# Normalising the next image on GpSimd in place of VectorE during attention

## The chip, the cores and the metric

The kernel runs on one core of one Trainium2 chip. Its time is the device time of one execution in microseconds (us), and the number compared is the median of several runs. The engines are TensorE (PE in the profile; PEld is its weight load), VectorE (DVE), ScalarE (ACT), GpSimd (POOL) and SyncE (SP), which issues most of the DMAs. Each engine works through its own queue in order; they wait for one another on semaphores.

## The reference

Sixteen images of 192 channels by 32 by 32 go through a convolutional attention block, then as 1024 tokens of 192 channels each through causal attention over 6 heads, and then through a mixture of 4 experts, of which each token takes 2. Every step adds its result to its input. What the change touches is the first line of it:

```python
mu = jnp.mean(x, axis=(1, 2, 3), keepdims=True)
var = jnp.mean((x - mu) ** 2, axis=(1, 2, 3), keepdims=True)
xn = (x - mu) * jax.lax.rsqrt(var + EPS) * ln_g + ln_b
Q = _proj(xn, wq_p, bq_p, wq_d, bq_d)   # 3x3 convolution per channel behind a head-wise product
...
out = jnp.einsum('bhnc,bhcd->bhnd', V, attn)
...
return jnp.einsum('bcij,oc->boij', out, w_f) + b_f[None, :, None, None] + xn
# then, on tokens:
t = t + _L1_attn_ref(_ln_t(t), L1_attn_W_qkv, L1_attn_W_proj, L1_attn_b_proj)
t = t + _L1_ffn_ref(_ln_t(t), L1_ffn_gate_w, L1_ffn_gate_b, L1_ffn_w1, L1_ffn_b1, L1_ffn_w2, L1_ffn_b2)
```

`ln_g` and `ln_b` have one value for each channel and pixel; the mean and the variance are one number for an image.

## The kernel before

A loop over the 16 images computes the convolution block and the attention of one image after the other; behind it a loop over 67 blocks of 512 routed rows computes the experts. An image takes about 133 us. The change lies in the loop over images.

**Stages of an image.** TensorE convolves the padded image (`conv`, L1720) from `ring`, which holds shifted copies of it. The padded image `xpad` (96 partitions, two halves of the channels, rows of 34 pixels) is written to DRAM by SyncE (`write_scratch`, L343) and read back in 36 shifted loads (`load_pairs`, L352). After the channel attention and its projection come the token norm, queries, keys and values, and then the token attention.

**The token attention** is an order written out by hand: 48 units, 8 chunks of 128 queries (`qc`, 0 to 7) times 6 heads (`h`), numbered n = 6 qc + h. For a unit, TensorE computes the scores (L1843, mask L1845), VectorE their negated row maximum (`score_max`, L1094), ScalarE the exponentials with row sums (L1543), TensorE transposes them (`blocks`, L1855), ScalarE or VectorE copies them out of PSUM (L1557, L1107). Scores run two or three units ahead. After h = 5 of a chunk TensorE multiplies by the values for four heads (`four_heads`, L1877), and in the next chunk at h = 1 for the last two (`two_heads`, L1887).

**The inverse sums.** VectorE takes the reciprocals of a chunk's row sums at the next chunk's h = 0 (`inverse_sums`, L1115). GpSimd copies them wide in two instructions (`inverse_wide`, L765 and L766), TensorE transposes these right behind `two_heads` (`norms`, L1895), ScalarE copies the result (L1565), VectorE multiplies (`weighted`, L1124), and at h = 3 TensorE projects (`output_projection`, L1904). "The third chunk's norms" below are those of qc = 2, executed in chunk qc = 3, and so on.

**The next image's norm** is woven into this attention on VectorE, by unit: statistics at n = 6 to 12, the deviation at 15, the variance at 18, with one small matrix product each on TensorE. GpSimd takes the reciprocal root (`image_rstd`, L390) behind the inverse sums of qc = 2. Then VectorE runs `gain` (L941), (x - mean) x ln_g in place, for either half at n = 20 and 22, and `shift` (L954), x rstd + ln_b into the inside of `xpad`, at n = 25 and 27. Each is one scalar_tensor_tensor over 96x1024 elements. SyncE's next steps after its loads for the attention are the two scratch writes and the 36 ring loads; the convolution of the next image starts behind unit 47. GpSimd copies `xpad` to `xn` (`unpad_image`, L328) at the next image's start.

In the last image (number 15, counted from 0) there is no next image: none of this work exists, and GpSimd instead splits expert weights behind the inverse sums (`split_behind`, L773 and L776).

Of the kernel before, what the change touches and what calls it, by code (L numbers as in the profile page):

```python
# [10 lines left out]
ALU = mybir.AluOpType  # L11
# [8 lines left out]
def hybrid_block_kernel(nc, x, ln_g, ln_b, conv_w, conv_bias_row, conv_taps, conv_bias, alpha_rows, w_f_t, b_f,  # L20
                        w_qkv_a, w_qkv_b, w_proj, w_proj_t, b_proj, gate_w_a, gate_w_b, gate_b, w1_a, w1_b, b1_t,
                        w2, b2, out):
    B, C, SH, SW = x.shape
# [51 lines left out]
    with ExitStack() as ctx:  # L75
# [29 lines left out]
        x_sb = at("x_sb", [HALF, 2, N], F32, 2 * (PAIRS - 1) * RING)  # L105
# [42 lines left out]
        img = sb("img", [HALF, 8])  # L148
# [122 lines left out]
        def sem(name):  # L271
            return ctx.enter_context(nc.semaphore(name))
# [30 lines left out]
        bcur_sb, xT_ps, xT_hi, xT_lo, up_ps, gelu_sb, lo_sb, down_ps, acc_ps, y_acc, yrow_sb = sems(  # L303
            "bcur_sb xT_ps xT_hi xT_lo up_ps gelu_sb lo_sb down_ps acc_ps y_acc yrow_sb")
        outT_ps, outs_sb, comb = sems("outT_ps outs_sb comb")
        w_hi, front_sb = sem("w_hi"), sem("front_sb")
        xgt_ld = [sem(f"xgt_ld{n}") for n in range(3)]
        cur_ld = [sem(f"cur_ld{n}") for n in range(2)]
        yrow_st = [sem(f"yrow_st{n}") for n in range(2)]
# [8 lines left out]

        def interior(h):
            return xpad[:, h, 0:PW * (SH + 2)].rearrange("p (a b) -> p a b", b=PW)[:, 1:SH + 1, 1:SW + 1]  # L320

        def unpad_image(pool, i):

# [64 lines left out]
        def image_rstd(pool, i):  # L388
            pool.wait_ge(img_veps, i + 1)
            nc.gpsimd.tensor_tensor(img[:, 5:6], img[:, 4:5], minus_half[0:HALF, 0:1], ALU.pow).then_inc(img_rstd, 1)  # L390
# [63 lines left out]
        def passage(i):  # L454
            return PASSAGES[0 if i + 1 < B else 1]

        def pass_bank(t):
            return 4 + t % 2
# [228 lines left out]
        def _(pool):  # L687
# [132 lines left out]
            def output_bias(i, j):  # L820
# [2 lines left out]
                g.tensor_tensor(t_sb[:, ch, :], t_sb[:, ch, :],  # L823
                                b2p_bc[:, :].unsqueeze(1).to_broadcast([P, TPC, CE]), ALU.add).then_inc(tb_sb, 1)

            for i in range(B):
                unpad_image(pool, i)
                if i:
                    send(i - 1, 0, 3)
                token_rstd(i, 0)  # L830
                if i:
                    send(i - 1, 3, 5)
                token_rstd(i, 1)
                if i:
                    send(i - 1, 5, 6)
                pool.wait_ge(qk_hi, NQ * i + PAIR_GROUPS)
                for j in range(2):
                    load_queries(g, 0, j, 0, QKh)
                    load_queries(g, 0, j, 2, QKh)
                pool.wait_ge(qk_lo, NQ * i + PAIR_GROUPS)  # L840
                for j in range(2):
                    load_queries(g, 0, j, 1, QKl)
                if i:
                    send(i - 1, 6, NC)
                output_bias(i, 0)
                for qc in range(NC):
                    inverse_wide(i, qc)
                    if qc == 0:
                        output_bias(i, 1)
                    if qc == 2 and i + 1 < B:  # L850
                        image_rstd(pool, i + 1)
                    if qc == TPC:
                        token_rstd2(i, 0)
                    if i + 1 == B:
                        split_behind(qc)
                if i + 1 < B:
                    token_rstd2(i, 1)
# [47 lines left out]
        def _(dve):  # L905
# [28 lines left out]
            def variance(i, at_bank):  # L934
                dve.wait_ge(stat_ps, 2 * i + 2)
                v.tensor_scalar(img[:, 4:5], bank(at_bank)[0:HALF, 1:2], 1e-5, None, ALU.add).then_inc(img_veps, 1)

            def gain(i, h):
                if i == 0 and h == 0:
                    dve.wait_ge(w_ld["ln"], 32)  # L940
                v.scalar_tensor_tensor(out=x_sb[:, h, :], in0=x_sb[:, h, :], scalar=img[:, 0:1],  # L941
                                       in1=lng[:, h, :], op0=ALU.subtract, op1=ALU.mult).then_inc(xg_sb, 1)

            def shift(i, h):
                if h == 0:
                    dve.wait_ge(img_rstd, i + 1)
                    dve.wait_ge(xg_sb, 2 * (i + 1))
                    if i:

                        dve.wait_ge(xn_flat, 2 * i)  # L950
                        for h2 in range(2):
                            dve.wait_ge(scr_w[h2], 16 * i)
                rows = lambda a: a.rearrange("p (a b) -> p a b", b=SW)
                v.scalar_tensor_tensor(out=interior(h), in0=rows(x_sb[:, h, :]), scalar=img[:, 5:6],  # L954
                                       in1=rows(lnb[:, h, :]), op0=ALU.mult, op1=ALU.add).then_inc(xn_sb, 1)

            for q in range(4):
                stats(0, q)
# [1 line left out]
            deviation(0, 4)  # L960
            variance(0, 4)
            for h in range(2):
                gain(0, h)
            dve.wait_ge(setup_pool, 4)
            for h in range(2):
                shift(0, h)
            dve.wait_ge(setup_pool, 7)
            v.tensor_copy(ident_g[:, 0:HALF], ident[0:HALF, 0:HALF])
            v.tensor_tensor(block_mask[:, :], mask_wide[:, 0:2 * W], mask_wide[:, 2 * W:P], ALU.max)
# [344 lines left out]
            for i in range(B):  # L1314
                conv_qk(i, 0)
                if i:
                    route(i - 1, 0)
                else:
                    finish_setup(0)
                conv_qk(i, 1)  # L1320
                if i:
                    route(i - 1, 1)
                else:
                    finish_setup(1)
                channel_logits(i, 0)
                if i:
                    route(i - 1, 2)
                else:
                    finish_setup(2)
                channel_attention(i, 0)  # L1330
                if i:
                    route(i - 1, 3)
                else:
                    finish_setup(3)
                conv_qk(i, 2)
                transposed_attention(i, 0)
                if i:
                    route(i - 1, 4)
                else:
                    finish_setup(4)  # L1340
                conv_qk(i, 3)
                channel_logits(i, 1)
                channel_attention(i, 1)
                if i:
                    route(i - 1, 5)
                transposed_attention(i, 1)
                if i:
                    route(i - 1, 6)
                else:
                    finish_setup(5)  # L1350

                for k in range(TPC):
                    channel_mixed(i, k)
                    if k:
                        first_stats(i, k - 1)
                first_stats(i, TPC - 1)
                channel_mixed(i, TPC)
                first_stats(i, TPC)
                normed(i, 0)
                for k in range(TPC + 1, NC - 1):  # L1360
                    channel_mixed(i, k)
                    first_stats(i, k)
                low_channels(i, 0)
                channel_mixed(i, NC - 1)
                first_stats(i, NC - 1)
                low_qk(i, 0)
                normed(i, 1)
                for n in range(1, QK_FIRST):
                    low_qk(i, n)
                low_channels(i, 1)  # L1370
                for n in range(QK_FIRST, NQ):
                    low_qk(i, n)

                image_steps = {6: lambda: stats(i + 1, 0), 8: lambda: stats(i + 1, 1), 10: lambda: stats(i + 1, 2),
                               12: lambda: (stats(i + 1, 3), partition_mean(i + 1)),
                               15: lambda: deviation(i + 1, pass_bank(passage(i).stat[0])),
                               18: lambda: variance(i + 1, pass_bank(passage(i).stat[1])),
                               20: lambda: gain(i + 1, 0), 22: lambda: gain(i + 1, 1),
                               25: lambda: shift(i + 1, 0), 27: lambda: shift(i + 1, 1)}
                def query_chunk(qc, stage):  # L1380
                    if stage == 0:
                        inverse_sums(i, qc)
                    if stage == 2:
                        weighted(i, qc)
                    if stage == 4:
                        attended(i, qc)
                    if stage == 5:
                        second_stats(i, qc)

                for n in SCORED_FIRST:  # L1390
                    score_max(i, n)
                for n, (qc, h) in enumerate(SOFT):
                    for m in SCORED[n]:
                        score_max(i, m)
                    blocks_out(i, n)
                    if qc:
                        query_chunk(qc - 1, h)
                    if i + 1 < B and n in image_steps:
                        image_steps[n]()
                    if i + 1 == B and n == 40:  # L1400
                        second_normed(i, 0)
                for stage in range(H):
                    query_chunk(NC - 1, stage)
# [748 lines left out]
```

## Time and profile before

| what | value |
|---|---|
| median of 3 runs | 3315.94 us (3314.32 to 3317.31) |
| profiled execution | 3319.14 us, span of its trace 3317.3 us |
| TensorE busy | 3075.1 us (93%) |
| VectorE busy | 2204.9 us (66%) |
| ScalarE busy | 1871.7 us (56%) |
| GpSimd busy | 875.3 us (26%) |
| mean granted TensorE clock | 0.986 of full |

Times inside the trace are counted from the span's start. The loop over images ends near 2225 us; the experts fill the rest. Image 14's attention runs from about 2000 to 2080 us, image 15's from about 2139 to 2222 us. "Releaser" is what ended an engine's idle time, read from semaphore events. The ends of matrix products are modelled, so starts are the firmer numbers.

### The profile page before, as it was taken

To read this page: it belongs to the slowest core of one execution; us is meant where nothing else is said; L and a number is where in the kernel's file an instruction comes from. 1 tells how busy PE (TensorE), PEld (TensorE's weight loads), DVE (VectorE), ACT (ScalarE), POOL (GpSimd) and SP (SyncE) were. 2 spreads that over 40 slices of the span, in tenths; PEclk is the share of its full clock that TensorE was granted. 3 is DMA by queue.
4 is the path that set the end of the run, shared out by engine and by line. 5 is a ranking of instruction groups with operands and counts; after the bars stand their busy time and mean duration, and the time that the engine had idled before them with its cause. 6 is when DMAs were issued, how large, how long until landed. Compare 5 with 4: busy or idle time off the path is not lost.

```text
span 3317.3 us, 72524 instructions
## 1 busy us (share of the span) xinstructions
PE 3075.1 (93%) x26642; PEld 2349.3 (71%) x26642; DVE 2204.9 (66%) x5632; ACT 1871.7 (56%) x3996; POOL 875.3 (26%) x1142
## 2 busy tenths in 40 slices
PE   4999999999989999999999999988999999999995
PEld 1666667666666676666766666667888888888884
DVE  3777677677776777777767777664565655655653
ACT  0647466475474664745746547464555555555553
POOL 2121303313123032131330322352133233233223
PEclk9999999999999999999999999999999999999997
DMA  7547445454464554644545447334667767767673
GB/s 178 142 113 174 123 115 149 123 156 119 124 165 115 136 138 115 173 115 126 150 124 148 127 113 183 100 130 147 187 219 221 216 202 217 216 209 225 202 215 118
DMA packets 256517, 519.83 MB, mean 157 GB/s; under 512 B 70919, under 2 KB 161991, under 8 KB 246521
## 3 DMA queue, kind: packets, MB, share of 16 engines
q1 hardware_dynamic: 222878, 453.58, 48.7%
q0 software_dynamic: 29184, 59.81, 6.0%
q8 instruction: 217, 3.56, 0.4%
q10 hardware_dynamic: 4107, 1.81, 0.3%
q14 instruction: 131, 1.07, 0.1%
HBM read 242.82 MB, written 117.71 MB: 109 GB/s over the span
## 4 chain that ended last, share of the span: by engine, by line
PE 67%; DVE 14%; issue 10%; ACT 3%; POOL 2%; DMA 2%; SPq 1%; DVEq 0%; ACTq 0%; POOLq 0%
PE ps L2042 13%; PE ps L1855 9%; PE ps L2058 9%; PE ps L1720 5%; PE ps L1843 5%; PE ps L2063 5%; PE ps L1804 3%; PE ps L1877 3%; PE ps L1887 2%; PE ps L2018 2%; PE ps L1812 2%; ACT p_sb L1543 2%; DVE minus_max L1094 1%; PE ps L1895 1%; PE ps L2027 1%
## 5 line engine op out<-in xcount | busy, mean ns | idle before, releaser
L1094 DVE TENSOR_REDUCE minus_max<-ps 128x1 f32<-128x128 f32 (+7 forms) x768 | 571.7, 750 | 246.9 <-PE ps L1845 231.3
L1543 ACT ACTIVATE p_sb<-ps,minus_max 128x128 f32<-128x128 f32 (+7 forms) x768 | 569.3, 741 | 41.0 <-DVE minus_max L1094 37.0
L1855 PE MATMUL ps<-ident,p_sb 128*128 128x128 f32 x3456 | 532.1, 279 | 44.5 <-ACT p_sb L1543 19.1
L1665 ACT ACTIVATE g<-ps,bcur 128x512 f32<-128x512 f32 x402 | 276.8, 688 | 447.4 <-PE ps L2042 441.4
L1428 DVE TENSOR_TENSOR g_lo<-g,g_hi 128x512 fp32r<-128x512 f32 x402 | 282.2, 702 | 361.4 <-ACT g_hi L1666 361.4
L1557 ACT ACTIVATE PT<-ps 128x512 f32<-128x512 f32 (+3 forms) x768 | 396.8, 517 | 134.4 <-PE ps L1855 125.3
L1855 PEld LDWEIGHTS ps<-ident,p_sb 128*128 128x128 f32 x3456 | 371.8, 142 | 99.4 <-ACT p_sb L1543 38.4
L2058 PE MATMUL ps<-w_all,g_hi 128*128 x1608 | 437.1, 352 | 1.6 <-DVE y_rows L1452 1.6
L1843 PE MATMUL ps<-KS,QS 96*128 96x512 f32 (+3 forms) x1152 | 393.6, 401 | 21.2 <-ACT p_sb L1543 19.6
L1720 PE MATMUL ps<-ring,wconv 125*32 125x512 f32 (+1 forms) x3072 | 357.1, 605 | 16.6 <-DMA ring<-padded_scratch 16.6
L817 POOL DMA_INDIRECT routed_rows<-xhat,slot x256 | 253.8, 991 | 345.6 <-issue 345.6
L878 POOL DMA_INDIRECT got<-expert_rows,slot x256 | 258.2, 1008 | 327.1 <-issue 267.9
L765 POOL COPY inverse_wide<-inverse_sums 128x192 f32<-128x192 f32 x128 | 44.2, 345 | 1046.7 <-DVE inverse_sums L1115 1046.7
L2063 PE MATMUL ps<-w_all,g_lo 128*128 x1608 | 292.6, 264 | 0.3 <-DVE g_lo L1428 0.3
L2063 PEld LDWEIGHTS ps<-w_all,g_lo 128*128 128x128 f32 x1608 | 289.8, 188 | 3.1 <-DVE g_lo L1428 1.2
L2058 PEld LDWEIGHTS ps<-w_all,g_hi 128*128 128x128 f32 x1608 | 264.4, 191 | 26.6 <-DVE y_rows L1452 2.3
L2042 PE MATMUL ps<-X_hi,cur 128*128 128x512 f32 x780 | 256.6, 410 | 18.9 <-issue 12.1
L1666 ACT ACTIVATE g_hi<-ps,bcur 128x512 fp32r<-128x512 f32 x402 | 273.4, 680 | 0.0
L1843 PEld LDWEIGHTS ps<-KS,QS 96*128 96x128 f32 x1152 | 196.9, 195 | 68.9 <-ACT p_sb L1543 41.7
L2042 PE MATMUL ps<-X,cur 128*128 128x512 f32 x780 | 244.9, 395 | 0.0
L1720 PEld LDWEIGHTS ps<-ring,wconv 125*32 125x32 f32 (+1 forms) x3072 | 93.5, 111 | 208.5 <-issue 193.1
L1107 DVE COPY PT<-ps 128x128 f32<-128x128 f32 (+3 forms) x384 | 184.9, 481 | 68.5 <-PE ps L1855 68.3
(293 smaller groups left out, 5462.7 us busy)
## 6 DMA issues: line engine op xcount, KB each, us to landing
ring<-padded_scratch SPq DMA_DIRECT2D x576, 204.0 KB
cur<-w_all SPq DMA_DIRECT2D x65, 1536.0 KB, 7.1
routed_rows<-zero_rows SPq DMA_DIRECT2D x67, 384.0 KB, 5.1
xgt<-routed_rows SPq DMA_DIRECT2D x67, 384.0 KB, 4.5
expert_rows<-y_rows SPq DMA_DIRECT2D x67, 384.0 KB, 3.1
padded_scratch<-xpad SPq DMA_DIRECT2D x32, 435.0 KB, 3.6
x_sb<-x SPq DMA_DIRECT2D x16, 768.0 KB, 5.4
KS<-QKh SPq DMA_DIRECT2D x128, 96.0 KB
```

Of the source, the lines that this page charges most:

```text
L1094: v.tensor_reduce(nmx[:, qc, h:h + 1], score_place(n), AX, ALU.max, negate=True).then_inc(mx_sb, 1)
L1428: v.tensor_tensor(g_lo[:, n % 2, :], g32[:, n % 2, :], g_hi[:, n % 2, :].bitcast(F32), ALU.subtract).then_inc(lo_sb, 1)
L1543: a.activation(p_sb[n % NP][:, 0:P * (qc + 1)], score_place(n), ACT.Exp, bias=nmx[:, qc, h:h + 1], accum_out=ls[:, qc, h:h + 1]).then_inc( ...
L1557: a.activation(PT[h][:, k0:k0 + nb, :], bank(pass_bank(t))[:, 0:P * nb].rearrange("p (k q) -> p k q", q=P), ACT.Copy).then_inc(PT_act, 1)
L1665: a.activation(g32[:, n % 2, :], bank(n % 2), ACT.Gelu, bias=b1)
L1666: a.activation(g_hi[:, n % 2, :], bank(n % 2), ACT.Gelu, bias=b1).then_inc(gelu_sb, 1)
L1720: last = t.matmul(bank(2 * (r % 2) + nh)[W * j:W * (j + 1), :], wconv[s][0:KROWS[s], h, c0:c0 + W], rhs, start=s == 0, stop=s == 1, skip_g ...
L1843: t.matmul(o[:, k0:k0 + keys], QS[0:96, qc // TPC, h, P * (qc % TPC):P * (qc % TPC + 1)], KS[0:96, h, k0:k0 + keys], start=True, stop=k0 + ...
L1855: last = t.transpose(bank(pass_bank(piece))[:, P * k:P * (k + 1)], p_sb[n % NP][:, P * (k0 + k):P * (k0 + k + 1)], ident[:, :])
L2042: last = t.matmul(bank(n % 2), w[:, W1L * part + P * j:W1L * part + P * (j + 1)], act_part[:, :], start=m == 0, stop=m == 4)
L2058: t.matmul(bank(acc_bank(r, tt))[:, 0:2 * C], g_hi[:, n % 2, P * tt:P * (tt + 1)], w2j, start=j == 0, stop=False, skip_group_check=True)
L2063: last = t.matmul(bank(acc_bank(r, tt))[:, 0:C], g_lo[:, n % 2, P * tt:P * (tt + 1)], w2j[:, 0:C], start=False, stop=j == J - 1, skip_grou ...
```

## The change

The four VectorE instructions for images 1 to 15 become six on GpSimd; for image 0 they stay (`first_gain`, `first_shift`). On GpSimd, `gain` stands behind the inverse sums of qc = 2 and the reciprocal root: for either half one tensor_scalar, (x - mean) x rstd in place, and one tensor_tensor, times ln_g in place, with a new semaphore `x_unit` between them. `shift` stands behind the inverse sums of qc = 3: for either half one tensor_tensor that adds ln_b and writes the inside of `xpad`. The waits of the old `shift` go along; each half now waits for its own scratch write.

```diff
+            def gain(i):
+
+                pool.wait_ge(xstat, 2 * i + 2)
+                pool.wait_ge(img_rstd, i + 1)
+                for h in range(2):
+                    g.tensor_scalar(x_sb[:, h, :], x_sb[:, h, :], img[:, 0:1], img[:, 5:6], ALU.subtract, ALU.mult
+                                    ).then_inc(x_unit, 1)
+                for h in range(2):
+                    pool.wait_ge(x_unit, 2 * (i - 1) + h + 1)
+                    g.tensor_tensor(x_sb[:, h, :], x_sb[:, h, :], lng[:, h, :], ALU.mult).then_inc(xg_sb, 1)
+
+            def shift(i):
+                pool.wait_ge(xg_sb, 2 * (i + 1))
+                pool.wait_ge(xn_flat, 2 * i)
+                for h in range(2):
+                    pool.wait_ge(scr_w[h], 16 * i)
+                    g.tensor_tensor(interior(h), image_rows(x_sb, h), image_rows(lnb, h), ALU.add).then_inc(xn_sb, 1)
...
                     if qc == 2 and i + 1 < B:
                         image_rstd(pool, i + 1)
+                        gain(i + 1)
+                    if qc == 3 and i + 1 < B:
+                        shift(i + 1)
...
-                               18: lambda: variance(i + 1, pass_bank(passage(i).stat[1])),
-                               20: lambda: gain(i + 1, 0), 22: lambda: gain(i + 1, 1),
-                               25: lambda: shift(i + 1, 0), 27: lambda: shift(i + 1, 1)}
+                               18: lambda: variance(i + 1, pass_bank(passage(i).stat[1]))}
```

## Rows read from the trace of the kernel before

**Rows 1.** The page: busy us (share of the span); the chain by engine
```profile
PE 3075.1 (93%) x26642; PEld 2349.3 (71%) x26642; DVE 2204.9 (66%) x5632; ACT 1871.7 (56%) x3996; POOL 875.3 (26%) x1142
...
PE 67%; DVE 14%; issue 10%; ACT 3%; POOL 2%; DMA 2%; SPq 1%; DVEq 0%; ACTq 0%; POOLq 0%
```

**Rows 2.** Windows (images 14, 14, 15): length, busy us of each engine, clock, DMA
```profile
2020.10:2029.20 9.10, 8.29 (x96) 6.28 (x94) 7.82 (x15) 8.03 (x20) 0.53 (x2) 1.00 0.00 1
2029.20:2039.90 10.70, 9.98 (x120) 7.90 (x116) 10.16 (x21) 8.82 (x20) 1.29 (x3) 1.00 0.56 148
...
2175.20:2183.00 7.80, 7.42 (x100) 5.84 (x99) 5.98 (x15) 6.31 (x13) 4.37 (x6) 1.00 0.01 2
```

**Rows 3.** Chain of waits in image 14: start us, us, what
```profile
2024.51 1.19 DVE x_sb L941
```

**Rows 4.** Timeline of TensorE, image 14: start us, us, what, idle before
```profile
2020.10 0.44 PE L1895 MATMUL ps<-ident,inverse_wide 128*128 128x128 f32 x2
...
2027.40 0.56 PE L1843 MATMUL ps<-KS,QS 96*128 96x512 f32 x2 [0.15 <-ACT p_sb L1543]
...
2028.65 0.64 PE L1887 MATMUL ps<-PT,v_sb 128*32 128x128 f32 x16
2029.22 0.44 PE L1895 MATMUL ps<-ident,inverse_wide 128*128 128x128 f32 x2
...
2032.06 0.50 PE L1904 MATMUL ps<-wproj_a,aT 128*128 128x196 f32 x2
...
2039.90 0.44 PE L1895 MATMUL ps<-ident,inverse_wide 128*128 128x128 f32 x2
```

**Rows 5.** Timeline of TensorE, image 15
```profile
2157.14 0.44 PE L1895 MATMUL ps<-ident,inverse_wide 128*128 128x128 f32 x2
...
2165.62 0.64 PE L1887 MATMUL ps<-PT,v_sb 128*32 128x128 f32 x16
2171.11 0.69 PE L1895 MATMUL ps<-ident,inverse_wide 128*128 128x128 f32 x2 [4.84 <-POOL inverse_wide L766]
...
2175.16 0.50 PE L1904 MATMUL ps<-wproj_a,aT 128*128 128x196 f32 x2
...
2183.00 0.44 PE L1895 MATMUL ps<-ident,inverse_wide 128*128 128x128 f32 x2
```

**Rows 6.** Groups by form, VectorE: shapes, count, busy us, mean ns, idle before
```profile
L954 DVE SCALAR_TENSOR_TENSOR xpad<-x_sb,img,lnb 96x1024 f32<-96x1024 f32 x32 | 40.8, 1277 | 0.1
L941 DVE SCALAR_TENSOR_TENSOR x_sb<-x_sb,img,lng 96x1024 f32<-96x1024 f32 x32 | 40.7, 1273 | 2.0 <-DMA lnb<-ln_b 2.0
```

**Rows 7.** Timeline of GpSimd, image 14
```profile
2019.36 0.58 POOL L390 TENSOR_TENSOR img<-img,minus_half 96x1 f32<-96x1 f32 x1
2027.99 0.35 POOL L765 COPY inverse_wide<-inverse_sums 128x192 f32<-128x192 f32 x1 [8.05 <-DVE inverse_sums L1115]
```

**Rows 8.** Groups by form, GpSimd
```profile
L328 POOL COPY xn<-xpad 96x1024 f32<-96x1024 f32 x32 | 32.3, 1036 | 0.1
...
L776 POOL TENSOR_TENSOR w_all<-w_raw,w_all 128x768 fp32r<-128x768 f32 x8 | 14.5, 1816 | 0.6
L776 POOL TENSOR_TENSOR w_all<-w_raw,w_all 128x1152 fp32r<-128x1152 f32 x4 | 10.6, 2642 | 0.3
...
L740 POOL TENSOR_SCALAR_AFFINE_SELECT mask_wide<-mask_wide 128x128 f32<-128x128 f32 x1 | 0.3, 308 | 0.1
```

**Rows 9.** Timeline of GpSimd, image 15
```profile
2170.53 0.34 POOL L765 COPY inverse_wide<-inverse_sums 128x192 f32<-128x192 f32 x1
2170.82 0.24 POOL L766 COPY inverse_wide<-inverse_sums 128x64 f32<-128x64 f32 x1
```

**Rows 10.** Timelines of SyncE and TensorE: ring loads, and their first reader
```profile
2034.18 22.31 SPq L352 DMA_DIRECT2D ring<-padded_scratch  x36
...
2069.91 1.50 PE L1720 MATMUL ps<-ring,wconv 125*32 125x512 f32 x12
```

**Rows 11.** Window with the granted clock (last but two), image 15
```profile
2172.00:2175.00 3.00, 3.00 (x16) 2.62 (x15) 2.22 (x4) 2.36 (x6) 2.92 (x2) 0.50 0.45 128
```

More of the change, by code:

```diff
@@ L305, in hybrid_block_kernel @@
         outT_ps, outs_sb, comb = sems("outT_ps outs_sb comb")
-        w_hi, front_sb = sem("w_hi"), sem("front_sb")
+        w_hi, front_sb, x_unit = sem("w_hi"), sem("front_sb"), sem("x_unit")
         xgt_ld = [sem(f"xgt_ld{n}") for n in range(3)]
@@ L320, in interior, with image_rows @@
             return xpad[:, h, 0:PW * (SH + 2)].rearrange("p (a b) -> p a b", b=PW)[:, 1:SH + 1, 1:SW + 1]
+        def image_rows(of, h):
+            return of[:, h, :].rearrange("p (a b) -> p a b", b=SW)
         def unpad_image(pool, i):
@@ L936, in variance, with first_gain @@
                 v.tensor_scalar(img[:, 4:5], bank(at_bank)[0:HALF, 1:2], 1e-5, None, ALU.add).then_inc(img_veps, 1)
-            def gain(i, h):
-                if i == 0 and h == 0:
+            def first_gain(h):
+                if h == 0:
                     dve.wait_ge(w_ld["ln"], 32)
@@ L942, in gain, with first_shift @@
                                        in1=lng[:, h, :], op0=ALU.subtract, op1=ALU.mult).then_inc(xg_sb, 1)
-            def shift(i, h):
+            def first_shift(h):
                 if h == 0:
[L946 to L955, printed above, removed]
+                    dve.wait_ge(img_rstd, 1)
+                    dve.wait_ge(xg_sb, 2)
+                v.scalar_tensor_tensor(out=interior(h), in0=image_rows(x_sb, h), scalar=img[:, 5:6],
+                                       in1=image_rows(lnb, h), op0=ALU.mult, op1=ALU.add).then_inc(xn_sb, 1)
             for q in range(4):
@@ L962, in _ @@
             for h in range(2):
-                gain(0, h)
+                first_gain(h)
             dve.wait_ge(setup_pool, 4)
             for h in range(2):
-                shift(0, h)
+                first_shift(h)
             dve.wait_ge(setup_pool, 7)
```

## The prediction

> **What bounds the kernel now.** I read the page's shares and its chain first, then the stretch of one image's attention in which the four VectorE instructions stand, and last the same stretch of the last image, which has no next image to normalise and so shows the kernel without them.
>
> The page shows TensorE busy 93% of the span, VectorE 66%, GpSimd 26%, and a chain that is 67% TensorE and 14% VectorE [rows 1]. Shares of the whole span say nothing of one stretch, so I take the windows around the four instructions in image 14's attention. From one chunk's norm transposes to the next, VectorE is busy 7.82 of 9.10 us where the gains stand and 10.16 of 10.70 us where the shifts stand, TensorE 8.29 and 9.98 [rows 2]. The chain of waits even runs through one of the four: 1.19 us on L941 at 2024.51, followed by the row maximum that ScalarE's exponential waits for [rows 3]. Read by itself this promises 1.19 us an image. But a chain shows one path that ended last, not by how much: where it returns to TensorE, at 2027.40, TensorE's own timeline says it had been idle only 0.15 us [rows 4]. Its work of the chunk before had nearly filled the time.
>
> The last image settles it. From the norm transposes of the third chunk (L1895) to the last two heads of the fourth (L1887), TensorE takes 2028.65 - 2020.10 = 8.55 us in image 14, with two gains on VectorE, and 2165.62 - 2157.14 = 8.48 us in image 15, without any [rows 4, 5]. From the output projection of that chunk (L1904) to the next norm transposes it takes 2039.90 - 2032.06 = 7.84 us with the shifts and 2183.00 - 2175.16 = 7.84 us without. So TensorE and its round trips set the pace, and VectorE's full windows are work that just fits.
>
> **The change, part by part.**
>
> *Removed from VectorE.* Two gains of 1.273 us and two shifts of 1.277 us for each of 15 images (the 32 counted in either row hold two of image 0, which stay) [rows 6]: 5.10 us an image, 76.5 us in all. The two comparisons above price it: 0.07 us in the gains' part, 0.00 in the shifts' part. Between L1887 and L1904 image 15 can't be compared (GpSimd held it up, below). There the bounds are 0 and all of TensorE's idle time from 2029.20 to 2039.90, 10.70 - 9.98 = 0.72 us [rows 2]; I take 0, as the rest of that stretch gave nothing. So 0.07 an image, bounds 0.07 and 0.79; 15 x 0.07 = 1.05 us.
>
> *Added on GpSimd, the gain.* It stands behind the reciprocal root of the image, which ends at 2019.36 + 0.58 = 2019.94, and ahead of the inverse-sum copies of the fourth chunk, which now start at 2027.99 [rows 7]. The new part is two scale-and-shift instructions with one tensor input (tensor_scalar) and two multiplications of two tensors, each 96x1024. For the multiplications the rows are GpSimd's TENSOR_TENSOR: 1.816 us for 768 elements, 2.642 us for 1152 [rows 8], so 2.15 ns an element and 2.37 us for 1024 (an estimate from these two). The one-input instruction is not in the trace. Its lower bound is the copy of 96x1024, 1.036 us; its upper bound is the two-input instruction, 2.37 us. I take 1.04 us, since the row nearest in kind is another instruction that computes on one tensor input, AFFINE_SELECT of 128 elements at 0.308 us, which lies between the copies of 64 and 192 elements at 0.24 and 0.34 us [rows 8, 9]. For the waits inside the gain I allow 0.2 us, my estimate. Sum: 2019.94 + 0.2 + 2 x 1.04 + 2 x 2.37 = 2026.95. That is 1.0 us before the inverse-sum copies are due, so nothing becomes later.
>
> How much could it grow? The wait added is no new wait in TensorE's program; what is queued behind the gain on GpSimd are the two copies of inverse_wide, and TensorE's norms wait for these, with ScalarE's norm copy, VectorE's weighted heads and the next exponentials behind. TensorE wants them at 2029.22 - 0.07 = 2029.15 [rows 4]. In image 15 they run from 2170.53 to 2171.06 and L1895 follows at 2171.11 [rows 5, 9]: 0.53 us for both and 0.05 to TensorE. They may start as late as 2028.57. From 2019.94 that leaves 8.63 us for the gain, or (8.63 - 0.2 - 4.74) / 2 = 1.85 us for each one-input instruction. Cost below that: nothing.
>
> The Trainium skill speaks against the move ("GPSIMD Engine Reference", Elementwise - side-by-side cycle accounting): GpSimd's two-input addition takes 1.96 times VectorE's, since both operands come over one read port, and 4497 ns for 2048 elements. By that page's figures, 1.03 cycles an element at 1.2 GHz for a one-input body and half of 4497 ns for a two-input one, the gain would be an estimated 6.3 us. The rows give a like ratio (2.37 against 1.273 us, 1.86): the work gets longer, but it moves to where 8.63 us are free.
>
> *Added on GpSimd, the shift.* Two additions, taken at 2.37 us each (the strided side of xpad costs the copy of L328 nothing visible: 1.036 us for 1024 elements). They start behind the copies of the fourth chunk, at 2028.6, and end at 2031.0 and 2033.4; GpSimd's next copies are wanted at TensorE's norm transposes of 2039.90 [rows 4], 6 us later. On SyncE the two scratch writes and the 36 ring loads follow the shifts; now the loads go out from 2034.18 in 22.31 us, and TensorE first wants a ring at 2069.91 [rows 10]. Even if the loads moved by the whole length of both additions, 4.7 us, they would be out at 2061.2. Cost starts 13 us after today's last issue; below that none.
>
> *Waits.* The gain's waits (deviation, rstd, its own x_unit) are for things done before 2019.94 or one instruction back. The shift's waits for the scratch writes and the unpadded copy are for those of the image before. They add a few tenths inside the slack above.
>
> **The sum.** Profiled execution: 3319.14 us with a span of 3317.3 us; 3319.14 - 1.05 = 3318.1. The median of the runs shown, 3315.94, lies 3.2 us below the profiled one; the same change gives 3314.9, and I write 3315.
>
> **Rivals.**
>
> *Faster: VectorE's relief reaches the path.* For it: the chain's 1.19 us and the two full windows. If all of it came back, 15 x 1.19 = 17.9 us, so 3298; all of TensorE's idle time in both stretches, 0.81 + 0.72 = 1.53 us [rows 2], would give 23 us, 3293, and is the most there is. Against it: image 15, where 5.1 us less of VectorE gave 0.07. Chance 0.10.
>
> *Slower: the gain outlasts its 8.63 us.* One place, the norm transposes of the fourth chunk in 15 images. At 2.37 us for the one-input instruction the gain ends at 2029.62, the copies at 2030.15, TensorE goes on at 2030.20 instead of 2029.15: 1.05 us, 15.8 us in all, so 3331. It decides from 1.85 us an instruction. For it: image 15 shows the very thing. GpSimd splits weights ahead of the same copies, they start at 2170.53, and TensorE stands 4.84 us for them [rows 5, 9]. After that stop the granted clock is 0.50 in the window from 2172 to 2175, the lower level of 1.2 GHz [rows 11]; whether a stop of 1 us brings that too no row shows, so the price may be higher. Against it: the rows chosen above for the two kinds of instruction, with 1.6 us to spare. Chance 0.10.
>
> *Slower: the two engines get in each other's way.* If VectorE's remaining 7.82 - 2.54 = 5.28 us of work in the 9.10 us stretch [rows 2] had to queue with GpSimd's 7 us, it would need 12.3 us, 3.2 more than there are; 15 x 3.2 = 48 us, so 3363. Against it: in image 15 GpSimd is busy 4.37 of the 7.80 us from 2175.20 on [rows 2], mostly with weight splits, and TensorE's 7.84 us there are those of image 14 to the hundredth. The Trainium skill ("GPSIMD Engine Reference", Specifications) says that GpSimd shares its SBUF interfaces with VectorE, and that contention comes with VectorE instructions of two SBUF inputs or in a two-port mode. The only ones here with two large SBUF inputs are the four that leave. Chance 0.02.
>
> **Chances and range.** No change 0.78, faster rival 0.10, slower ones 0.12. What can be told from no change is 0.2%, 6.6 us: 3309.3 to 3322.6. The forecast's own range is 3311 to 3320: the three runs of the kernel before lie 3 us apart. To leave out no more than 2 in 10 I reach into the slower case up to an instruction of 2.2 us (15 x 2 x 0.35 = 10 us) and into half of the faster: 3307 to 3325. Of the 0.78, 0.01 falls outside on either side: faster 0.11, same 0.76, slower 0.13.
>
> **What would show it.** After: six GpSimd instructions an image, one-input ones near 1.04 us, two-input ones near 2.37; L766's copies of the fourth chunk ending at least 0.05 us ahead of the norm transposes; VectorE busy down by 76 us to about 2128 [rows 1]; the distance from image to image unchanged within 0.1 us; the ring loads landed long before the convolution. It is wrong if the distance between images shrinks by 0.5 us or more (relief counts), or if TensorE waits for inverse_wide in the fourth chunk.

## The result and the profile after

The changed kernel takes 3392.68 us (median of 5 runs, 3389.22 to 3394.65), the kernel before 3315.94 us in the runs beside it: ratio 1.0228, 95% interval 1.0217 to 1.024. That is slower by 76.7 us, 5.1 us for each of the 15 images that have a next one. Forecast was no change.

The page of the changed kernel: busy us and share of the span (3392.8 us), then the chain by engine.

```profile
PE 3101.6 (91%) x26642; PEld 2377.7 (70%) x26642; DVE 2140.3 (63%) x5572; ACT 1872.6 (55%) x3996; POOL 1131.1 (33%) x1232
...
PE 64%; DVE 12%; issue 10%; POOL 8%; DMA 2%; ACT 2%; SPq 1%; DVEq 0%; ACTq 0%; POOLq 0%
```

Against [rows 1], GpSimd's part of the chain rises from 2% to 8%. TensorE is busy 26.5 us more with the same 26642 instructions, and its mean granted clock over the span falls from 0.986 to 0.975. VectorE's sixty instructions have left. Now the new instructions, GpSimd's groups by form: shapes, count, busy us in all, mean ns of one, idle before.

```profile
L834 POOL TENSOR_SCALAR x_sb<-x_sb,img 96x1024 f32<-96x1024 f32 x30 | 113.4, 3781 | 2.9 <-POOL img L393 2.8
L845 POOL TENSOR_TENSOR xpad<-x_sb,lnb 96x1024 f32<-96x1024 f32 x30 | 70.3, 2360 | 0.0
L838 POOL TENSOR_TENSOR x_sb<-x_sb,lng 96x1024 f32<-96x1024 f32 x30 | 69.6, 2335 | 0.0
```

The two-input ones cost what was forecast (2.37 us). The one-input one takes 3.78 us, not 1.04, and lies above the bound of 2.37. Image 14 on GpSimd's timeline (start us, us, what, idle before) shows where that goes:

```profile
2091.20 0.58 POOL L393 TENSOR_TENSOR img<-img,minus_half 96x1 f32<-96x1 f32 x1
2091.96 7.56 POOL L834 TENSOR_SCALAR x_sb<-x_sb,img 96x1024 f32<-96x1024 f32 x2 [0.19 <-POOL img L393]
2099.50 4.63 POOL L838 TENSOR_TENSOR x_sb<-x_sb,lng 96x1024 f32<-96x1024 f32 x2
2104.09 0.33 POOL L768 COPY inverse_wide<-inverse_sums 128x192 f32<-128x192 f32 x1
2104.37 0.23 POOL L769 COPY inverse_wide<-inverse_sums 128x64 f32<-128x64 f32 x1
```

The reciprocal root ends at 2091.78, the copies were due 8.63 us later at 2100.41, and they start at 2104.09: 3.68 us late. TensorE in the same stretch, answering to [rows 4] (L1895, L1887 and L1904 are now L1911, L1903 and L1920):

```profile
2091.94 0.44 PE L1911 MATMUL ps<-ident,inverse_wide 128*128 128x128 f32 x2
...
2100.42 0.64 PE L1903 MATMUL ps<-PT,v_sb 128*32 128x128 f32 x16
...
2104.65 0.69 PE L1911 MATMUL ps<-ident,inverse_wide 128*128 128x128 f32 x2 [3.58 <-POOL inverse_wide L769]
2108.32 0.50 PE L1920 MATMUL ps<-wproj_a,aT 128*128 128x196 f32 x2
...
2116.16 0.44 PE L1911 MATMUL ps<-ident,inverse_wide 128*128 128x128 f32 x2
```

From the third chunk's norms to the fourth's it now takes 12.71 us instead of 9.12. From the fourth's to the fifth's, where no wait was added, it takes 11.51 instead of 10.68. The windows say why (length, busy us of PE, PEld, DVE, ACT and POOL, granted clock, DMA share, GB/s):

```profile
2102.00:2105.00 3.00, 0.35 (x3) 0.35 (x3) 0.00 (x0) 0.00 (x0) 3.00 (x4) 0.91 0.00 0
2105.00:2108.00 3.00, 3.00 (x16) 2.54 (x15) 1.68 (x4) 2.27 (x5) 3.00 (x2) 0.52 0.10 31
2108.00:2111.00 3.00, 2.76 (x22) 2.34 (x21) 2.21 (x6) 2.59 (x7) 1.26 (x1) 1.00 0.74 203
```

In the first window GpSimd alone works until TensorE's last 0.35 us. In the second TensorE is back, but the granted clock is 0.52, near the lower level of 1.2 GHz, where the kernel before had 1.00 [rows 2]. It does 16 instructions in 3.00 us and 22 in 2.76 us in the next one. The loss lies where the clock is low: L1911 to L1920 takes 2108.32 - 2104.65 = 3.67 us where the kernel before took 2.84, and from L1920 to the next norms it is 7.84 us in both [rows 4].

Over all 15 images the first stretch grew by 54.0 us in all (about 3.60 each) and the second by 23.0 us (1.53 each). The granted clock falls in all 15: in image 14 it is low for 3.3 us of the second stretch, in six others for 3.4 us, and in the remaining eight for 5.0 to 6.5 us, which lose 1.7 to 2.4 us each. Together the two stretches give 77.0 us, against 75.5 between the two profiled executions and 76.7 in the medians, so no other place has to be looked for.

### The profile page after: what moved, and what is told of

Its sections match the earlier page's. It is cut to its first block, busy times and chain, and to the rows that moved or that the text cites. A ratio compares the mean times of both kernels' runs of the same rounds, so it can differ in the third digit from the quotient of the medians.

```text
span 3392.8 us, 72554 instructions
## 1 busy us (share of the span) xinstructions
PE 3101.6 (91%) x26642; PEld 2377.7 (70%) x26642; DVE 2140.3 (63%) x5572; ACT 1872.6 (55%) x3996; POOL 1131.1 (33%) x1232
## 3 DMA queue, kind: packets, MB, share of 16 engines
q14 instruction: 131, 1.07, 0.1%
## 4 chain that ended last, share of the span: by engine, by line
PE 64%; DVE 12%; issue 10%; POOL 8%; DMA 2%; ACT 2%; SPq 1%; DVEq 0%; ACTq 0%; POOLq 0%
PE ps L2058 13%; PE ps L2074 8%; PE ps L1871 8%; PE ps L1736 5%; PE ps L1859 5%; PE ps L2079 5%; POOL x_sb L834 3%; PE ps L1820 3%; PE ps L1893 3%; PE ps L1828 2%; PE ps L2034 2%; PE ps L1911 1%; PE ps L1903 1%; ACT p_sb L1559 1%; POOL x_sb L838 1%
## 5 line engine op out<-in xcount | busy, mean ns | idle before, releaser
L1871 PE MATMUL ps<-ident,p_sb 128*128 128x128 f32 x3456 | 546.7, 285 | 48.7 <-ACT p_sb L1559 18.6
L1871 PEld LDWEIGHTS ps<-ident,p_sb 128*128 128x128 f32 x3456 | 382.9, 145 | 104.6 <-issue 38.6
L1859 PE MATMUL ps<-KS,QS 96*128 96x512 f32 (+3 forms) x1152 | 404.6, 411 | 14.2 <-ACT p_sb L1559 12.6
L1736 PE MATMUL ps<-ring,wconv 125*32 125x512 f32 (+1 forms) x3072 | 357.8, 604 | 19.3 <-DMA ring<-padded_scratch 19.1
L2074 PEld LDWEIGHTS ps<-w_all,g_hi 128*128 128x128 f32 x1608 | 264.5, 191 | 26.5 <-DVE y_rows L1468 2.4
L2058 PE MATMUL ps<-X_hi,cur 128*128 128x512 f32 x780 | 256.6, 410 | 18.4 <-issue 12.2
L1859 PEld LDWEIGHTS ps<-KS,QS 96*128 96x128 f32 x1152 | 205.4, 203 | 55.4 <-ACT p_sb L1559 28.3
```

The costliest lines, as they stand in the source:

```text
L1736: last = t.matmul(bank(2 * (r % 2) + nh)[W * j:W * (j + 1), :], wconv[s][0:KROWS[s], h, c0:c0 + W], rhs, start=s == 0, stop=s == 1, skip_g ...
L1859: t.matmul(o[:, k0:k0 + keys], QS[0:96, qc // TPC, h, P * (qc % TPC):P * (qc % TPC + 1)], KS[0:96, h, k0:k0 + keys], start=True, stop=k0 + ...
L1871: last = t.transpose(bank(pass_bank(piece))[:, P * k:P * (k + 1)], p_sb[n % NP][:, P * (k0 + k):P * (k0 + k + 1)], ident[:, :])
L2058: last = t.matmul(bank(n % 2), w[:, W1L * part + P * j:W1L * part + P * (j + 1)], act_part[:, :], start=m == 0, stop=m == 4)
L2074: t.matmul(bank(acc_bank(r, tt))[:, 0:2 * C], g_hi[:, n % 2, P * tt:P * (tt + 1)], w2j, start=j == 0, stop=False, skip_group_check=True)
```

## The experiments

The lines of each kernel's helpers differ by a few, so the norms' TensorE line is named where it is shown.

**Spread: the same instructions, the gain split over two chunks.** The one-input instructions stay behind the third chunk's copies, the multiplications go behind the fourth's, the shift behind the fifth's.

```
                 if qc == 2: gain(i + 1)         # now the two tensor_scalar alone
+                if qc == 3: times_gain(i + 1)   # the two multiplications
-                if qc == 3: shift(i + 1)
+                if qc == 4: shift(i + 1)
```

> The six GpSimd instructions stay but are spread: the two one-input ones (3.78 us each in the changed kernel) behind the third chunk's inverse sums, the two multiplications behind the fourth's, the two additions behind the fifth's. Theory (GpSimd's gain of 12.2 us outlasts the 8.6 us until the fourth chunk's norm transposes, TensorE stands 3.6 us and loses some 1.5 us more to the lower clock): 7.6 + 0.3 us fits 8.6, so all of it goes and the time is that of the kernel before, 3313 to 3317 us. Rival (GpSimd's work slows VectorE wherever it stands, or the later scratch writes cost): the 11.8 us an image are all still there, so the time stays near 3390, or at least above 3335.

Measured 3314.97 us against 3318.08, ratio 0.999 [0.9981, 0.9999]. The whole loss is gone, with every instruction still on GpSimd (busy 1132.4 us, 1131.1 in the changed kernel). Its timeline and TensorE's norms in image 14:

```profile
2018.96 7.57 POOL L834 TENSOR_SCALAR x_sb<-x_sb,img 96x1024 f32<-96x1024 f32 x2 [0.19 <-POOL img L393]
2026.83 0.35 POOL L768 COPY inverse_wide<-inverse_sums 128x192 f32<-128x192 f32 x1 [0.30 <-DVE inverse_sums L1137]
...
2027.31 4.69 POOL L840 TENSOR_TENSOR x_sb<-x_sb,lng 96x1024 f32<-96x1024 f32 x2
```

```profile
2018.94 0.44 PE L1915 MATMUL ps<-ident,inverse_wide 128*128 128x128 f32 x2
...
2028.00 0.44 PE L1915 MATMUL ps<-ident,inverse_wide 128*128 128x128 f32 x2
```

GpSimd is 0.30 us ahead of the inverse sums, and the stretch takes 9.06 us (9.12 before). The length of the work in front of the copies is the cause, not the engine that does it nor a quarrel over memory, for GpSimd is as busy here as in the changed kernel.

**The one-input instructions alone back on VectorE**, at units 20 and 22 of the image's steps; multiplications and shifts stay on GpSimd.

```
-    g.tensor_scalar(x_sb[:, h, :], x_sb[:, h, :], img[:, 0:1], img[:, 5:6], ALU.subtract, ALU.mult
+    20: lambda: unit(i + 1, 0), 22: lambda: unit(i + 1, 1)   # the same as v.tensor_scalar
```

> Only the one-input instruction goes back to VectorE (units 20 and 22, where the gains stood); the multiplications and additions stay on GpSimd where the change put them. Theory: the 7.6 us of one-input instructions are the whole excess, so 3313 to 3318 us. Rival (any two-input GpSimd work between the chunks costs): at least 15 us above the kernel before.

Measured 3318.67 against 3318.08, ratio 1.0 [0.9986, 1.0013]. The loss is gone again, so it was these two instructions' 7.56 us. The shift still stands behind the fourth chunk's copies here, and the stretch behind them takes its old 10.68 us, so the shift had no part in the second stretch's loss. On VectorE their timeline shows two durations for one form:

```profile
2025.18 0.80 DVE L961 TENSOR_SCALAR x_sb<-x_sb,img 96x1024 f32<-96x1024 f32 x1
...
2027.76 1.31 DVE L961 TENSOR_SCALAR x_sb<-x_sb,img 96x1024 f32<-96x1024 f32 x1
```

GpSimd's multiplication of the first half, on its own timeline, runs across the second:

```profile
2026.15 2.37 POOL L835 TENSOR_TENSOR x_sb<-x_sb,lng 96x1024 f32<-96x1024 f32 x1 [2.87 <-DVE x_sb L961]
```

It ends at 2028.52, VectorE's instruction 0.55 us later at 2029.07. So the longer duration seems to hold a wait for the other engine; the splits of the last image, below, bear this out.

**Widths: how much earlier is early enough?** Three kernels narrow the one-input instruction; the other columns of images 1 to 15 aren't centred and scaled.

```
-    g.tensor_scalar(x_sb[:, h, :], x_sb[:, h, :], ...
+    g.tensor_scalar(x_sb[:, h, 0:N], x_sb[:, h, 0:N], ...   # N = 512, 640, 768
```

> The changed kernel with the one-input instruction over 512 of its 1024 columns; the other columns of images 1 to 15 are left unnormalised. Theory: price in proportion, near 1.95 us each, gain 3.9 + 4.7 + 0.3 = 8.9 us, 0.3 us late: 3315 to 3322 us. Rival (a fixed price per instruction, as for code that is loaded anew): each still over 3 us, TensorE stands over 2 us an image, 3350 us or more.

> The changed kernel with the one-input instruction over 640 columns (the other columns of images 1 to 15 unnormalised), to see what a stop of about 1 us costs beyond itself. Price 0.37 + 640 x 3.33 ns = 2.50 us each, stop 0.24 + 2 x 0.43 = 1.1 us an image. If the clock stays at 1.00: 3316 + 15 x 1.1 = 3333 us; if it falls as after the stop of 1.9 us (1.36 us more in the next chunk): 3353.

> The same over 768 columns. Theory: near 2.87 us each, gain 5.75 + 4.7 + 0.3 = 10.7 us, TensorE stands 2.1 us an image, 15 x 2.1 = 32 us, and less or nothing for the clock if a stop of 2 us does not lower it: 3347 us; with the clock's 1.5 us as well 3369. Rival (fixed price): near 3390.

| columns | one instruction | norms 3 to 4, sum of 15 images | norms 4 to 5, sum of 15 | time, and before | ratio |
|---|---|---|---|---|---|
| 0 (before) | | 136.7 us | 160.2 us | | |
| 512 | 2.073 us | 140.2 | 160.2 | 3320.81, 3318.08 | 1.0009 [0.9996, 1.0021] |
| 640 | 2.500 us | 152.9 | 160.2 | 3331.55, 3317.52 | 1.0045 [1.0028, 1.0062] |
| 768 | 2.926 us | 165.5 | 182.7 | 3363.14, 3318.08 | 1.0132 [1.0116, 1.0148] |
| 1024 | 3.781 us | 190.7 | 183.2 | 3392.68, 3315.94 | 1.0228 [1.0217, 1.024] |

The two columns of norms are sums over the starts of the norm transposes on TensorE's timeline in the profiled execution; the times are medians. The wait alone grows evenly with the instruction: 3.5, 16.2, 28.8 and 54.0 us, which is 30 times what is over some 1.97 us an instruction, close to the prediction's 1.85. With 640 columns it is the whole loss. From 768 on some 22.5 us come on top in the next chunk (28.8 + 22.5 = 51.3, the profiled execution being 48.7 us over that of the kernel before). These go with the clock. With 640 columns, TensorE's fourth and fifth norms and a window behind them:

```profile
2042.75 0.44 PE L1911 MATMUL ps<-ident,inverse_wide 128*128 128x128 f32 x2 [1.07 <-POOL inverse_wide L769]
...
2053.43 0.44 PE L1911 MATMUL ps<-ident,inverse_wide 128*128 128x128 f32 x2
```

```profile
2043.00:2046.00 3.00, 2.67 (x21) 2.18 (x20) 2.25 (x5) 2.74 (x7) 3.00 (x2) 1.00 0.11 26
```

With 768:

```profile
2076.79 0.44 PE L1911 MATMUL ps<-ident,inverse_wide 128*128 128x128 f32 x2 [1.91 <-POOL inverse_wide L769]
...
2088.83 0.44 PE L1911 MATMUL ps<-ident,inverse_wide 128*128 128x128 f32 x2
```

```profile
2079.00:2082.00 3.00, 3.00 (x14) 2.67 (x12) 1.12 (x2) 2.06 (x5) 2.38 (x2) 0.57 0.50 149
```

After a stop of 1.07 us the granted clock stays 1.00 and the chunk takes its usual 10.68 us. After 1.91 us it is 0.57, and the chunk takes 12.04 us in this image and 12.18 on average. It is so in every image: with 640 columns the clock stays at 1.00 and the chunk takes 10.68 us in all 15, with 768 the clock falls in all 15. Between the two stops the price of a stop jumps by 1.5 us.

**The relief alone.** The kernel before with VectorE's gains and shifts of images 1 to 15 cut to one row of 32 pixels (the rest stays unnormalised), nothing on GpSimd.

```
+    w = SW if i else N      # gain over w columns
+    w = 1 if i else SH      # shift over w rows
```

> The kernel before, with VectorE's two gains and two shifts of images 1 to 15 over one row of 32 pixels only; the rest of these images is left unnormalised. Nothing is added on GpSimd. It measures what VectorE's relief alone is worth. Theory (TensorE sets the pace, the relief is worth 0.07 us an image, at most a few tenths): 1 to 5 us below the kernel before. Rival (the chain of waits is right, 1.19 us an image come back): 18 us below, 3298 us.

Measured 3316.71 against 3317.26, ratio 1.0003 [0.9994, 1.0013]. In image 14 the two stretches take 9.06 and 10.68 us: 0.06 us of relief in the first, none in the second, with the instruction down to 0.24 us. The 18 us of the faster rival are not there.

**What a one-input instruction costs on GpSimd.** Spread with another form of it in each of images 1 to 8, whose values then differ from the reference's. "Pointer" means that the scalar is read from a column of `img`, otherwise it is a constant.

```
+ 1: subtract, pointer    2: subtract 0.5, mult 1.5    3: subtract 0.5    4, 5: 512, 256 columns
+ 6: tensor_tensor(x, img[:, 0:1].to_broadcast)        7: mult, pointer   8: tensor_copy
```

> The spread kernel, with another form of the one-input GpSimd instruction in each of images 1 to 8 (their values are wrong from there): 1 one operation with a pointer scalar, subtract; 2 two operations with constants; 3 one operation with a constant; 4 and 5 the full form over 512 and 256 columns; 6 a two-input subtraction of the broadcast scalar; 7 one multiplication with a pointer scalar; 8 a copy; the rest as in spread. Theory A (each of the two operations costs a pass of its own, two cycles an element each): forms 1, 3 and 7 near 1.9 to 2.4 us, form 2 near 3.8. Theory B (it is the pointer scalars that cost): forms 2 and 3 near 1.1 us, 1 and 7 near 2 to 3.8. Theory C (TENSOR_SCALAR on GpSimd has one slow body whatever its operands): all near 3.8 us, and 512 and 256 columns at 2.07 and about 1.2 us. Form 6 at 2.35 us, form 8 at 1.04 us in any case. Its time says nothing but should stay under 3320 us.

The groups by form, in the order 2, 7, 1, 3, 4, 6, 5, 8, and the unchanged form:

```profile
L835 POOL TENSOR_SCALAR x_sb<-x_sb 96x1024 f32<-96x1024 f32 x2 | 7.3, 3642 | 0.2 <-POOL img L393 0.2
L840 POOL TENSOR_SCALAR x_sb<-x_sb,img 96x1024 f32<-96x1024 f32 x2 | 5.7, 2842 | 0.2 <-POOL img L393 0.2
L834 POOL TENSOR_SCALAR x_sb<-x_sb,img 96x1024 f32<-96x1024 f32 x2 | 5.7, 2841 | 0.2 <-POOL img L393 0.2
L836 POOL TENSOR_SCALAR x_sb<-x_sb 96x1024 f32<-96x1024 f32 x2 | 5.5, 2778 | 0.2 <-POOL img L393 0.2
L837 POOL TENSOR_SCALAR x_sb<-x_sb,img 96x512 f32<-96x512 f32 x2 | 4.1, 2072 | 0.2 <-POOL img L393 0.2
L839 POOL TENSOR_TENSOR x_sb<-x_sb,img 96x1024 f32<-96x1024 f32 x2 | 3.7, 1892 | 0.1
L838 POOL TENSOR_SCALAR x_sb<-x_sb,img 96x256 f32<-96x256 f32 x2 | 2.4, 1222 | 0.2 <-POOL img L393 0.2
L841 POOL COPY x_sb<-lng 96x1024 f32<-96x1024 f32 x2 | 2.0, 1038 | 0.1
L843 POOL TENSOR_SCALAR x_sb<-x_sb,img 96x1024 f32<-96x1024 f32 x14 | 53.0, 3783 | 1.3 <-POOL img L393 1.3
```

The full form goes by length: (3783 - 1222) / 768 = 3.33 ns a column and 0.37 us besides. A second operation adds 0.86 us with constants and 0.94 with pointers; pointers instead of constants add 0.06 to 0.14. Even the leanest form, one operation with a constant, costs 2.78 us, 2.7 times the copy. So none of the simple theories holds alone; nearest is a slow body of the instruction, to which a second operation adds a third. The same subtraction with the scalar broadcast as a second tensor takes 1.89 us. Two of these, one for each operation, would take an estimated 3.78 us, as much as the tensor_scalar with both: this spelling saves only where one operation is wanted.

**Where else the time could come from: image 15's weight splits.** [rows 5] show that the kernel before has a 4.84 us stop there. Its weight splits were moved to later chunks, once in the kernel before and once in spread (waits left out of the edit).

```
 if qc == 2:  - split_first(0, 0); split_first(0, 1)
 if qc == 3:  - split_second(0); split_first(1, 0)
              + split_first(0, 0); split_first(0, 1); split_first(1, 0)
 if qc == 4:  - split_first(1, 1); split_second(1)
              + split_second(0); split_first(1, 1); split_first(2, 0)
 if qc == 5:  - split_first(2, 0); split_first(2, 1); split_second(2)
              + split_second(1); split_first(2, 1); split_second(2)
 if qc == 6:  - split_second(3)
 if qc == 7:  + split_second(3)
```

> The kernel before, but in the last image GpSimd's first two weight splits stand behind the fourth chunk's inverse sums, not the third's, and the others follow in groups that fit between two chunks. The last image had TensorE stand 4.84 us before the fourth chunk's norm transposes, and its granted clock was 0.50 for a few us after it. Theory (the same mechanism as in the changed kernel, the price is the stop and the slower clock after it): 5 to 7 us below the kernel before, 3309 to 3311. Rival (the weights are wanted soon after, so the splits only move the wait to the experts' first blocks): no gain, 3316.

> The spread kernel with the late splits of the last image as well. Theory: both are free of stops, so the gains add: 3 us from the spreading, 5 to 7 from the splits, 3306 to 3310 us. Rival: VectorE's relief is nothing, then it equals late_splits alone.

Before with late splits took 3315.12 against 3317.26, ratio 0.9997 [0.9986, 1.0007]; spread with them 3312.17, ratio 0.9981 [0.9971, 0.999]. The two chunks' 13.97 and 11.89 us of image 15 became 9.06 and 10.68, 6.12 us less. But other waits of TensorE gave it back (what waits, for what: us in all, times, longest), here in before with late splits:

```profile
PE ps L2046 <- DMA cur<-w_all: 5.3, 1, 5.3
PE ps L1859 <- DVE PT L1111: 2.4, 2, 2.2
```

The last weights come 5.3 us late for the first expert matmuls, a wait that the kernel before doesn't have. The wait for VectorE's copies of `PT` is 2.4 us where it was 1.5. So 5.3 + 0.9 = 6.2 us are lost, as much as was won. In spread's version the stop for weights is 5.7 us.

**Late, but done one chunk sooner.** Against the late splits, the first part of the last expert's first layer is split behind the sixth chunk and the rest behind the seventh, with nothing behind the eighth; once on spread, once on before.

```
-    if qc == 6: split_first(3, 0); split_first(3, 1)
-    if qc == 7: split_second(3)
+    if qc == 5: ...; split_first(3, 0)
+    if qc == 6: split_first(3, 1); split_second(3)
```

> The spread kernel, the last image's splits regrouped once more: one first-layer split more behind the sixth chunk's sums, so that all of them end some 5 us earlier, near 2204 instead of 2210.8. In the kernels with late splits TensorE stood 5.3 and 5.7 us for the first experts' weights, whose copy goes out behind the last split. Theory (the 6.1 us won in the last image's attention were given back there): this stop goes too, 5 us less than spread_late, 3306 to 3309 us. Rival (the copy then waits for something else as late): no change from spread_late, 3312.

> The same splits in the kernel before, with its normalisation left on VectorE. Theory: 5 to 6 us below the kernel before, 3310 to 3312 us, and 1 to 2 us above spread_split2, since VectorE's relief is worth 0.1 us an image. Rival: no gain.

On spread 3310.92 against 3317.52, ratio 0.9981 [0.997, 0.9992]; on before 3318.01, ratio 1.0 [0.9987, 1.0013]. Both fell short. The weights' stop is gone, but TensorE has a new one of 4.3 us behind VectorE. TensorE's wait, VectorE's timeline and GpSimd's, all of spread's version:

```profile
PE ps L1878 <- DVE PT L1132: 4.3, 1, 4.3
```

```profile
2185.87 5.93 DVE L1170 TENSOR_SCALAR xhat<-t_sb,tmv,rstd 128x192 f32<-128x192 f32 x4
```

```profile
2186.35 2.65 POOL L779 TENSOR_TENSOR w_all<-w_raw,w_all 128x1152 fp32r<-128x1152 f32 x1
...
2189.88 1.80 POOL L779 TENSOR_TENSOR w_all<-w_raw,w_all 128x768 fp32r<-128x768 f32 x1
```

Four VectorE instructions, which take 0.37 us each in the fastest kernel below, take 5.93 us together with GpSimd's splits. Their durations are 0.52, 2.81, 0.87 and 1.96 us, and each ends 0.11 to 0.12 us after one of GpSimd's splits; the last at 2191.80, GpSimd's at 2191.68. In the kernel before, where one of GpSimd's splits ran beside them, the same four took 2.94 us:

```profile
2201.09 2.94 DVE L1145 TENSOR_SCALAR xhat<-t_sb,tmv,rstd 128x192 f32<-128x192 f32 x4
```

The rival that the prediction gave 0.02 is real; it sits in another place than feared.

**All of it together.** Spread, these splits, and the last image's four tensor_scalar from unit 40 to unit 46.

```
-    if i + 1 == B and n == 40:
+    if i + 1 == B and n == 46:
```

> The spread kernel with the regrouped splits, and in the last image VectorE's four normalising instructions of unit 40 moved to unit 46. In the kernel without this move they took 5.93 us in place of 1.2, each ending 0.1 us after a GpSimd instruction, and TensorE stood 4.3 us for the copy behind them. Theory (VectorE's one-input instructions and GpSimd's share a port and the later one waits for the whole of the earlier): at unit 46 GpSimd's splits are done, the four take 1.2 us, the stop of 4.3 us goes; 4 us below spread_split2, 3305 to 3309 us. Rival (VectorE is late at the end of the attention, and 1.2 us more there are on the path): 1 us above that.

Measured 3304.45 us (6 runs) against 3316.22, ratio 0.9961 [0.9947, 0.9976]: 11.8 us faster than the kernel before and 88 us faster than the changed one. VectorE's four are free of the splits:

```profile
2201.05 1.24 DVE L1170 TENSOR_SCALAR xhat<-t_sb,tmv,rstd 128x192 f32<-128x192 f32 x4
```

TensorE's longest wait for another engine from 2130 to 2220 is now 1.5 us.

One thing stays open. Three pairs of kernels differ in the spread normalisation alone, and the spread one is lower each time: by 3.1 us as it stands, by 3.0 with the late splits, by 7.1 with the regrouped ones. The relief of VectorE accounts for 0.9 us of it (15 x 0.06). The rest was found in no one place, and the last step was not run on the kernel before, so how much of the 11.8 us comes from the spreading isn't known.

## Why the prediction was wrong

*What bounds the kernel, and the relief of VectorE:* right. Image 15's comparison said 0.07 and 0.00 us. In the changed kernel L1911 to L1903 takes 2100.42 - 2091.94 = 8.48 us, image 15's figure to the hundredth; the relief alone gave 0.06 and 0.00. The chain's 1.19 us [rows 3] was worth nothing, as the last image without the work had shown.

*The two-input instructions:* right, 2.335 and 2.360 us for 2.37.

*The one-input instruction:* this is the step that failed, "I take 1.04 us", with "its upper bound is the two-input instruction, 2.37 us". It takes 3.781 us. The value came from AFFINE_SELECT of 128 columns, which is another operation: by the line fitted above, tensor_scalar would take an estimated 0.80 us for 128 columns, not 0.308. Even of that operation the prediction took the cheapest of the fp32 rows over this shape. The trace of the kernel before also has it at four times the price, and why isn't known:

```profile
L726 POOL TENSOR_SCALAR_AFFINE_SELECT earlier<-earlier 128x128 f32<-128x128 f32 x1 | 1.3, 1261 | 0.0
```

The upper bound rested on the belief that one tensor input can't cost more than two, which no row showed. With the measured 3.781 and 2.335 us in the prediction's own sum, 2019.94 + 0.2 + 7.56 + 4.67 = 2032.37, against a latest start at 2028.57: 3.80 us late, 57 us in all (54.0 measured). The mechanism was the rival "the gain outlasts its 8.63 us", whose deadline of 1.85 us nearly held: the widths put it at 1.97 us. The rival had a chance of 0.10, although that deadline lay inside the prediction's own bounds of 1.04 and 2.37 us.

The Trainium skill ("GPSIMD Engine Reference", Elementwise - side-by-side cycle accounting) spoke against the move, since GpSimd does such work more slowly than VectorE. That is so here: 12.2 us for a gain that took VectorE 2.55 us, though spread shows that the longer work need not cost time. The skill's 1.03 cycles an element for a body of up to two operations, at 1.2 GHz an estimated 0.86 ns, do not hold for this form. The copy's 1.038 us is near the estimated 0.88 us for 1024 columns, while tensor_scalar took 3.33 ns a column. So the gain that the skill's figures put at an estimated 6.3 us took 12.2. Measurement decides.

*The price of a stop:* "whether a stop of 1 us brings that too no row shows" was left at that. A stop of 1.07 us doesn't, 1.91 and 3.58 us do, and in the changed kernel this was 23.0 of the 77.0 us. For the stop that the rival had reckoned with, 1.05 us, its price was about right: the 640 columns, with a stop of 1.07 us, took 14.0 us more than the kernel before, for the rival's 15.8. The rival's 3331 us fell short because the instruction is longer than its upper bound.

*The engines in each other's way:* rightly small in this change, as spread and the old 10.68 us show. The prediction's reason was incomplete: it looked at VectorE instructions with two large inputs alone, and the traces show one-input ones held up as well. The Trainium skill ("SBUF — State Buffer", Who interferes with whom) says that whichever of a two-port VectorE instruction and a GpSimd one is issued first holds the shared ports for its whole length. The traces agree for tensor_scalar. In the splits it ends 0.12 us after GpSimd's instruction and takes 0.37 us alone; across GpSimd's multiplication it ended 0.55 us after it and takes 0.80 us alone. In either case some 0.25 us of it ran beside the other and the rest waited for the other's end. By the starts in the trace VectorE was 0.04 us ahead in two of the four cases in the splits and waited all the same, so the rule fits only if the ports are taken later than an instruction's start as shown.

*What would show it:* VectorE busy was to fall by 76 us to about 2128 and fell by 64.6 to 2140.3. The sixty instructions' durations did leave (their two groups are 76.4 us shorter), but busy time counts overlapping records once, and these overlapped with their neighbours: the trace of the kernel before, counted without the sixty, has VectorE busy 2137.2 us. The ring loads had room, as forecast: TensorE waited four times for them, 19.1 us in all, and all four lie in image 0, where the kernel before has four of 16.6 us.

## What to carry to other kernels

Before moving an operation, find that very operation on that very engine in a trace, or measure it. A row of another operation gives neither a value nor an upper bound, and if the deadline lies inside what is left possible, the slower rival deserves a large chance.

Work put ahead of a small instruction on an in-order engine is priced by its whole length against the time at which that small instruction is due. Split it so that each piece fits in front of one due time, as spread did, and the same work costs nothing.

A full engine isn't a bound: where a stretch of the same loop runs without the work, compare it before hoping for relief.

## What the runs showed of the hardware

- GpSimd's tensor_scalar on fp32 is dearer than its two-input multiplication: 3.78 us against 2.34 us for 96x1024, and 2.84 us with one operation against 1.89 us for the same subtraction with the scalar broadcast as a tensor.
- A stop of TensorE of 1.07 us left its granted clock at 1.00; after 1.91 us it was 0.57 in the 3 us shown behind it, after 3.58 us 0.52. The low clock cost between 0.83 and 2.36 us an image in the changed kernel, 1.53 on average: 0.83 to 1.11 us where it was low for 3.3 to 3.4 us of the chunk, 1.73 to 2.36 where it was low for 5.0 to 6.5. What decides how long it stays low isn't settled here.
- A VectorE tensor_scalar that meets a GpSimd instruction shows the wait inside its duration, not as idle time: 5.93 us for four instructions that took 1.24 in the fastest kernel. That shared ports are the reason is the word of the Trainium skill ("SBUF — State Buffer", Who interferes with whom) and fits the ends of both; it was not tested apart.
